# Issuing two thirds of a kernel's stores from ScalarE's queue instead of SyncE's

## What is computed

```
bilinear = einsum('bie,ied->bid', feature, weight)   # (2048, 200, 64)
out      = einsum('bid,bjd->bij', bilinear, feature) # (2048, 200, 200)
```

## Time and profile before

| | before |
|---|---|
| median of 3 runs | 1463.5 us (1458.56 to 1463.85) |
| the profiled execution, device time | 1465.03 us |
| its span, first to last instruction | 1463.2 us |
| mean granted TensorE clock | 0.993 |
| TensorE matmuls (PE) | 1330.3 us busy, 91% |
| VectorE | 985.6 us, 67% |
| ScalarE | 934.7 us, 64% |
| GpSimd | 306.5 us, 21% |
| moved by DMA | 438.55 MB, mean 300 GB/s |

### The profile page before, as it was taken

One profiled execution on the slowest core, in us unless ns is written; L12 is line 12 of the kernel. 1 busy time (PEld: TensorE's weight loads), 2 busy tenths in 40 slices (PEclk: granted clock), 3 DMA queues, 4 the chain that ended last, 5 costly groups with the idle time before them and its releaser, 6 DMA issues.

```text
span 1463.2 us, 39805 instructions
## 1 busy us (share of the span) xinstructions
PE 1330.3 (91%) x16192; PEld 1225.6 (84%) x16192; DVE 985.6 (67%) x1877; ACT 934.7 (64%) x1100; POOL 306.5 (21%) x518
## 2 busy tenths in 40 slices
PE   7999998999999988998999989999889999999974
PEld 7988888898888888888888878888879888889853
DVE  0667676667666766767676766766676767676785
ACT  5666666666666666766666666666666666666643
POOL 0112122222121212212221212222222222222221
PEclk9999999999999999999999999999999999999998
DMA  9799999999999999999999999999999999999998
GB/s 274 236 301 295 322 313 298 317 285 319 312 286 297 293 308 314 299 322 283 316 304 312 296 292 323 290 314 302 308 312 288 322 304 298 322 300 317 265 262 267
DMA packets 264788, 438.55 MB, mean 300 GB/s; under 512 B 51616, under 2 KB 250272, under 8 KB 252320
## 3 DMA queue, kind: packets, MB, share of 16 engines
q1 hardware_dynamic: 240032, 422.78, 88.9%
q0 software_dynamic: 24576, 13.24, 6.8%
HBM read 108.13 MB, written 327.68 MB: 298 GB/s over the span
## 4 chain that ended last, share of the span: by engine, by line
DMA 42%; PE 34%; SPq 9%; DVE 9%; ACT 3%; issue 3%; ACTq 0%; DVEq 0%; POOLq 0%
DMA out_dram<-staging 42%; PE ps L272 15%; PE ps L256 13%; SPq L194 8%; PE ps L244 6%; DVE staging L305 4%; ACT staging L305 3%; DVE win L357 2%; DVE win L365 1%; DVE win L364 1%; SPq L182 1%; DMA x<-feature_dram 1%; SPq L189 0%; ACT xt L318 0%; ACT bl L328 0%
## 5 line engine op out<-in xcount | busy, mean ns | idle before, releaser
L272 PE MATMUL ps<-win,bl 64*100 64x200 f32 x8192 | 771.2, 338 | 59.4 <-DVE staging L305 41.0
L272 PEld LDWEIGHTS ps<-win,bl 64*100 64x100 f32 x8192 | 697.8, 207 | 120.6 <-issue 64.2
L305 ACT COPY staging<-ps 100x800 f32<-100x800 f32 x683 | 548.2, 829 | 328.9 <-PE ps L272 169.8
L227 POOL DMA_DIRECT2D out_dram<-staging x512 | 305.8, 597 | 1146.1 <-ACT staging L305 910.4
L305 DVE COPY staging<-ps 100x800 f32<-100x800 f32 x341 | 335.2, 983 | 234.2 <-PE ps L272 206.8
L357 DVE COPY win<-xt 128x400 f32<-128x400 f32 x512 | 278.5, 544 | 208.7 <-PE ps L272 155.1
L256 PE MATMUL ps<-xt,w 64*64 64x128 f32 x6400 | 371.0, 271 | 15.2 <-DVE staging L305 9.9
L256 PEld LDWEIGHTS ps<-xt,w 64*64 64x64 f32 x6400 | 348.5, 133 | 33.4 <-issue 20.5
L328 ACT COPY bl<-ps 128x1024 f32<-128x1024 f32 (+1 forms) x208 | 202.3, 981 | 153.7 <-PE ps L256 153.7
L244 PE MATMUL ps<-ident,x 128*128 128x128 f32 x1600 | 205.0, 282 | 44.0 <-DVE staging L305 20.1
L244 PEld LDWEIGHTS ps<-ident,x 128*128 128x128 f32 x1600 | 179.2, 144 | 69.1 <-issue 60.4
## 6 DMA issues: line engine op xcount, KB each, us to landing
out_dram<-staging SPq DMA_DIRECT2D x1024, 300.0 KB, 7.6
x<-feature_dram SPq DMA_DIRECT2D x80, 1024.0 KB, 9.7
x<-feature_dram SPq DMA_DIRECT2D x16, 1280.0 KB, 9.7
out_dram<-staging POOLq DMA_DIRECT2D x512, 25.0 KB, 5.8
w<-weight_dram SPq DMA_DIRECT2D x24, 128.0 KB, 6.0
w<-weight_dram SPq DMA_DIRECT2D x2, 64.0 KB, 4.6
```

Source lines behind the costliest of these rows:

```text
L227: nc.gpsimd.dma_start(out_v[FA:FH, PB * (s - 1):PB * (s + 1), :], staging[FA:FH, slot - 1:slot + 1].rearrange("p s b h j -> p (s b) (h j)" ...
L272: last = nc.tensor.matmul(tile[0:FH, h, F * b:F * (b + 1)], row_of_bl(n, R * k + PB * i + b)[64 * h:64 * h + 64], win[64 * h:64 * h + 64, ...
L305: copy(staging[:, slot, :, :, :].rearrange("p b h j -> p h b j"), tile_of("scores", s)[0:FH, :, 0:PB * F].rearrange("p h (b j) -> p h b j" ...
```

## The change

ScalarE's own queue issues the stores of the sets that ScalarE copies. It does so after it has issued its next copy of a set, so that the store of set s stands behind the copy of the next set that isn't VectorE's. The store of the last set (1023, copied by ScalarE) comes at the very end. SP issues only the stores of VectorE's sets, and the loads of x at the places where they were. What is stored, from which slot, to where, and which semaphore counts it is unchanged, as are GpSimd's stores.

```diff
             for n in range(BLOCKS):
                 for s in range(SETS_B):
-                    store(n * SETS_B + s)
+                    if staged_by_dve(n * SETS_B + s):
+                        store(n * SETS_B + s)
                     if s - 2 in transposed_at:
@@ scalar
+            def store(s):
+                slot = s % OSLOTS
+                wait_staged(act, s)
+                act.dma_start(out_v[0:FA, PB * s:PB * (s + 1), :], staging[0:FA, slot]
+                              ).then_inc(out_written[slot], 16)
+
@@
                     if not staged_by_dve(n * SETS_B + s):
                         stage(act, nc.scalar.copy, staged_act, n * SETS_B + s)
+                        before = n * SETS_B + s - (2 if staged_by_dve(n * SETS_B + s - 1) else 1)
+                        if before >= 0:
+                            store(before)
                     if n + 1 < BLOCKS and s in transposed_at:
                         for u in BUNDLES[transposed_at[s]]:
                             store_xt(n + 1, u)
                     if n + 1 < BLOCKS and s in weighed_at:
                         for u in BUNDLES[weighed_at[s]]:
                             store_bl(n + 1, u)
+            store(BLOCKS * SETS_B - 1)
```

## The result

| | before | changed |
|---|---|---|
| median | 1461.5 us (4 runs, 1458.56 to 1463.85) | 1502.2 us (4 runs, 1492.81 to 1511.16) |
| ratio, 95% interval | | 1.0279 (1.0209 to 1.0348) |
| span of the profiled execution | 1463.2 us | 1503.1 us |
| mean granted TensorE clock | 0.993 | 0.989 |

The account below looks back on a forecast made before the run. The prediction took DMA as the bound, TensorE close behind. Its terms, +25 +27 -20 -2 = +30 us, gave 1495.0, adjusted to 1493.5 us; the forecast's own range was 1471 to 1530, the 8-in-10 range 1425 to 1545.

Parts of the forecast that it names:

- faster rival: Two queues relieve DMA, more GB/s in the middle blocks, shorter slot waits on ScalarE: 1428 us; chance of faster 0.33.
- Part A: ScalarE's queue: 683 store issues, some outlasting the copy beside them, delay TensorE; 0 to 49 us, taken as 25 slower.
- The share 0.21: Part of ScalarE's delay reaching TensorE, from 112.4 us of DMA waits against 8.0 + 15.7 us of TensorE's waits.
- Part B: Between runs of scores, 90 places: stores leave late and hold slots some 6.3 us; 0 to 82 us, taken as 27.
- DMA runs dry for one store each time: Upper bound for stores held back at 90 places between runs of scores: 0.91 us each, 82 us.
- the sign named for being wrong on B: DMA share at 0.97 or more between the runs of scores would refute Part B's 27 us.
- Part C: Loads of x and stores on separate queues mix reads and writes; gain of 0 to 66 us, taken as 20.
- Part D: Smaller things, chiefly the last store issued earlier at the kernel's end; 2 of 6 us taken as gain.
- TensorE 7% behind: Reading of the kernel before: DMA and TensorE close together as limits, TensorE 7% behind, kept apart by ten staging slots.

Follow-up runs that it names:

- k1_flush: Changed kernel, but stores held back between two runs of scores are issued by ScalarE behind its first copy to xt or bl there; 1490.8 us, ratio 1.0205.
- e5_half: k1_flush, but ScalarE issues only the stores of sets with s % 3 == 0 (342), SP the others; 1448.9 us, ratio 0.9902.
- k2_x_on_act: Kernel before, all 1024 stores on SP, but loads of x issued by ScalarE behind its copies to xt; 1448.6 us, ratio 0.9904.
- e8_small_issues: Kernel before, plus an 8 KB DMA on ScalarE's queue behind each of its 683 copies of scores; 1495.3 us, ratio 1.0223.
- e12: k1_flush, but ScalarE issues 513 of its 683 stores; 1440.3 us, ratio 0.9846.
- e6: k1_flush, but each store is issued right behind its own copy instead of one copy later; 1502.5 us, ratio 1.0272.
- e9: Kernel before, all stores on SP, with ScalarE sets' stores held back only at the 105 places between runs of scores; 1463.8 us, ratio 1.0012.
- k4: Kernel before with eight staging slots instead of ten; 1584.9 us, ratio 1.0856.
- k3: Kernel before, all stores on SP, which holds each ScalarE set's store until the scores of ScalarE's next set are done; 1493.5 us, ratio 1.0210.
- e10_x_on_act_later: k2_x_on_act, but ScalarE issues each load of x behind its copy of set s + 4; 1464.4 us, ratio 1.0015.
- e7: Kernel before, all on SP, with each load of x behind the store of set s instead of s + 2; 1477.7 us, ratio 1.0110.

## Why the prediction was right, and where its terms were off

**Direction and size.** Slower was forecast at 0.53, 1493.5 us within 1471 to 1530; 1502.2 us came, in the forecast's own range. ScalarE's issues with a median near 0.8 (749 ns), the DMA share near 0.95, and SP idle between its stores were named as signs, and all three are there. For the last, SP's own waits in the changed kernel (us in total, times, longest):

```profile
SPq L194 <- DVE staging L306: 1201.3, 336, 12.4
```

One sign of the faster rival came, too, ScalarE's shorter wait for slots (92.3 us, where it was 112.4), but VectorE's wait for slots rose from 2.3 to 19.5 us, and the GB/s didn't rise. Read on one engine alone, that sign says little:

```profile
ACT staging L306 <- DMA out_dram<-staging: 92.3, 44, 6.2
DVE staging L306 <- DMA out_dram<-staging: 19.5, 13, 4.4
```

**Part A was sized too low.** Its upper bound was 232 us of issues that outlast the copies, times 0.21, or 49 us; I took half. The trace of the changed kernel shows 242 us, the full bound and a little more, though the median issue is 749 ns and not 1170: the tail makes it up. With the places between runs mended (k1_flush) the kernel is 29 us slower; it also has the second queue, which is worth 12 to 14 us where ScalarE isn't blocked (e5_half, k2_x_on_act), so by difference the blocking costs some 41 to 42, if the second queue's gain holds beside a full one, which no run shows. The traces of e5_half and k1_flush, which differ in who issues 341 stores, show 28 us more waits of TensorE, all behind issues, and 16 us more busy time, which isn't explained.

The reason given for halving, that two stores in three and no loads fill a queue less often, failed: with all 683 stores ScalarE's queue is the one that stands, at 209.86 MB to SP's 212.92. In the three kernels of the first table the median issue is longer on the queue with more packets (142064 to 97968 here). Whether packets decide, or the number of stores, or how closely they follow each other, wasn't tried, and e8_small_issues, with long issues on a queue of few packets, doesn't fit.

The sign by which TensorE was to feel it, more than 24 us of waits for ScalarE's staging copies, is there: 14.9 + 10.8 + 6.7 = 32.4 us, where it was 23.7. Its waits for VectorE's, which no sign named, grew more, from 41.0 + 20.1 + 9.9 = 71.0 to 33.7 + 32.6 + 25.8 = 92.1:

```profile
PE ps L273 <- DVE staging L306: 33.7, 46, 2.0
PE ps L257 <- DVE staging L306: 32.6, 28, 2.6
...
PE ps L245 <- DVE staging L306: 25.8, 28, 2.7
...
PE ps L273 <- ACT staging L306: 14.9, 26, 1.6
...
PE ps L245 <- ACT staging L306: 10.8, 13, 2.7
...
PE ps L257 <- ACT staging L306: 6.7, 10, 1.9
```

The share 0.21 itself is no law. Of the issues that outlast their copies, what reaches TensorE by the table above is 25 of 242 us in the changed kernel (0.10), 29 of 216 in k1_flush (0.13), 5 of 95 in e12 (0.05) and 67 of 387 in e6 (0.17). So the 25 us that were taken are met by this count, and are too low by the difference of the runs.

**Part B was sized too high.** Taken at 27 us, it is 11 us by k1_flush (by my estimate -3 to 24), and 1.3 us (from -1.6 to 5.1 by the interval) by e9, where SP holds the stores. The bound "DMA runs dry for one store each time" didn't come true: in the two stretches at 662 us, between two runs of scores, the share is 1.01 and 1.03, the sign named for being wrong on B. What remained was the other half of the reason, slots that come free late: VectorE's waits for slots cost TensorE 54 us in the changed kernel and 16 in k1_flush. Waits elsewhere grew when these went, so the gain was smaller. What is right of it is the value of a slot: 61 us each between ten and eight (k4), and 31 us if all of ScalarE's sets go late on SP (k3).

**Part C was nearly right.** Taken at 20 us of gain, it measures 12 to 14 in two kernels where ScalarE isn't blocked; in the changed kernel itself it can't be read off. By the rule of the Trainium skill that was weighed against it ("DMA: Bandwidth & Descriptors", section "Issuing engines are not separate DMA queues") it is 0; k2_x_on_act and e5_half disagree with the rule here by 1%, with both intervals clear of 1, and e10_x_on_act_later, with a second queue and a ratio of 1.0015, agrees with it. Besides the queue, the place of the loads differs in k2_x_on_act, and in e5_half a third of the stores leaves one copy later. The reason given, reads and writes in two lines, isn't shown: e5_half gains with its loads still among SP's stores.

**Part D** had a tail of 2 us less. The last store is issued at 1495.1 of 1503.1 and before at 1458.1 of 1463.2: no gain there.

**The clock, and a misreading.** The prediction put the clock at nothing. The mean granted clock went from 0.993 to 0.989 and TensorE's busy time from 1330.3 to 1340.9 us, so a term of up to 11 us was missing. "TensorE 7% behind" DMA is misread, too: by the stages it was at 92 to 93% with DMA at 97%, 4 to 5 points behind.

**The sum.** 1 to 11 us for B, 41 for A and -13 for C give 29 to 39 us; 40.7 were measured. That the upper end comes near is no check, since A and B are differences of the same runs. The prediction's +30 was made of terms two of which were off by some 16 us, in opposite directions. Part of the good total is luck. How much of A is the blocked engine itself, and how much its stores' being one copy late inside a run of scores, wasn't tried apart on ScalarE's queue. That e12 issues 513 stores one copy late and still gains 22 us leaves little for the second, and e6 shows that a queue that stands can cost as much with no store late.

## What to carry to other kernels

A DMA issue on a compute engine's queue cost nothing here while it took 0.32 us beside a copy of 0.83. Where it took longer than the copy it blocked the engine's next work, and the busy share of the engine didn't show it (64% before, 62% after). With a DMA share of 0.93 to 0.98 in the middle of these kernels the stores' wait for room showed on one queue or the other. On SP's no compute stands behind it: see to it that the queue with the long issues is that one. Moving half to three quarters of ScalarE's stores gained 1.0 to 1.5%, and moving all of them lost 2 to 3%; compare the median issue time of both queues, and its tail, to see on which side one is. Before blaming an engine for a wait, check in the program's order which tile the waiting work needs and who empties it.

## What the runs showed of the hardware that was not expected

- A full queue of SP left ScalarE's issues of 300 KB stores short: 323 ns on ScalarE while SP's take 1171 (e5_half). With small DMAs of 16 rows the issues took 433 ns at the median and up to 2412, with little on their queue (e8_small_issues). This wasn't explained.
- Small packets are dear: 5.64 MB in 8 KB transfers took 1.9% of the 16 engines (28 us), where 422.78 MB take 88.9%; per byte that is 1.6 times as much.
- The place of the loads of x among the stores counts: loading two sets earlier on SP costs 16 us (e7), four sets later on ScalarE 16 us against its own earlier place (e10).
- TensorE's granted clock fell after a pause at 662 us: 0.97 us of work in the 3.5 us before 668.5, then a granted clock of 0.50 (1.2 GHz) at 669 to 672. The changed kernel's TensorE is busy for 1340.9 us against 1330.3 with the same 16192 matmuls, and some of the loss may be this. Busy time doesn't follow the clock alone, though: e6_own_store has 1362.8 us at a mean clock of 0.994. With eight slots the mean clock is 0.970.
